# Six slots for expert tiles and three for second-layer weights, with the tile loop unrolled by six

## What is computed

```
h = tok(x)                            # 16-step patches, stride 8: 92 tokens a sample, width 128
h = h + attn(layernorm(h))            # 8 heads, keys and queries 64 wide, values 128 wide
t = layernorm(h)                      # over the 128 values of a token
gates = softmax(t @ Wr + br)          # 8 experts, the best 2 kept, scaled to a sum of 1
for e in range(8):
    out += combine[:, e] * (relu(t @ W1[e] + b1[e]) @ W2[e] + b2[e])    # hidden width 512
h = h + out
```

## Time and profile before

| | us |
|---|---|
| median of three runs | 1813.76 |
| the three runs | 1808.7 to 1816.97 |
| the profiled execution | 1818.27 |
| its span, first to last instruction | 1816.4 |

### The profile page before, as it was taken

How to read it: one execution, slowest core, us unless ns; L and a number is a source line. 1 busy time by engine, 2 the same in 40 slices (tenths; PEclk the granted TensorE clock), 3 DMA queues, 4 the chain that set the end, 5 groups by cost and what they waited for, 6 DMA issues and landing times.

```text
span 1816.4 us, 33518 instructions
## 1 busy us (share of the span) xinstructions
PE 1560.2 (86%) x8364; PEld 1258.9 (69%) x8364; DVE 1166.5 (64%) x2839; ACT 1050.4 (58%) x2345; POOL 767.5 (42%) x884
## 2 busy tenths in 40 slices
PE   6689999999999999999878889889668888888840
PEld 4568887888788878887667677767546667666630
DVE  3557888788888888888756665655535555455532
ACT  2457777777777777777645555454334444444410
POOL 1453333333333332333266555555625455455444
PEclk9889999999999999999987887887779999999975
DMA  3312222222222222222375445445246556566558
GB/s 75 105 63 76 79 75 91 75 79 75 91 75 79 75 91 75 79 75 83 134 260 185 157 166 187 168 155 185 69 166 206 199 199 209 194 209 207 189 185 299
DMA packets 144102, 247.31 MB, mean 136 GB/s; under 512 B 23856, under 2 KB 86976, under 8 KB 144064
## 3 DMA queue, kind: packets, MB, share of 16 engines
q1 hardware_dynamic: 112784, 204.37, 32.1%
q0 software_dynamic: 15008, 34.34, 5.6%
q10 hardware_dynamic: 16272, 8.15, 1.6%
HBM read 100.78 MB, written 90.43 MB: 105 GB/s over the span
## 4 chain that ended last, share of the span: by engine, by line
PE 54%; issue 15%; DVE 10%; POOL 9%; DMA 7%; ACT 3%; SPq 2%; another core or an unknown queue 0%; POOLq 0%; DVEq 0%; ACTq 0%
PE bank L308 11%; PE bank L310 9%; PE bank L309 9%; PE bank L1338 6%; PE bank L1400 4%; PE bank L1268 4%; PE bank L1366 3%; DMA w2t<-w2s 2%; POOL y_scratch L691 2%; DMA y_scratch<-ytok,tin 2%; POOL rstdA L565 2%; POOL sorted_scratch L663 1%; DVE aT_l L1060 1%; PE bank L1259 1%; DVE total L1007 1%
## 5 line engine op out<-in xcount | busy, mean ns | idle before, releaser
L558 POOL TENSOR_TENSOR prob<-expo,inv 92x368 f32<-92x368 f32 x256 | 205.0, 801 | 520.7 <-DVE inv L1017 520.7
L691 POOL DMA_INDIRECT y_scratch<-ytok,tin x212 | 202.9, 957 | 231.8 <-DVE ytok L1222 154.8
L1213 DVE SCALAR_TENSOR_TENSOR hid_l<-bank,hid_h 128x512 fp32r<-128x512 f32 x212 | 146.2, 691 | 190.0 <-ACT hid_h L902 119.7
L902 ACT ACTIVATE hid_h<-bank 128x512 fp32r<-128x512 f32 x212 | 126.2, 598 | 205.9 <-PE bank L310 156.9
L663 POOL DMA_INDIRECT sorted_scratch<-trow,posi x184 | 180.7, 982 | 145.2 <-DVE posi L1139 87.4
L1338 PE MATMUL bank<-z,xnT 128*92 128x368 f32 x512 | 203.2, 479 | 0.0
L1060 DVE TENSOR_TENSOR aT_l<-bank,aT_h 128x512 fp32r<-128x512 f32 x184 | 125.8, 691 | 113.0 <-ACT aT_h L839 84.4
L1041 DVE TENSOR_TENSOR w2s<-bank,w2s 128x368 fp32r<-128x368 f32 x256 | 136.8, 534 | 69.6 <-ACT w2s L794 69.6
L1012 DVE TENSOR_REDUCE peak<-bank 92x4 f32<-92x368 f32 x256 | 136.1, 532 | 69.6 <-PE bank L1338 69.4
L839 ACT ACTIVATE aT_h<-bank 128x512 fp32r<-128x512 f32 x184 | 109.0, 598 | 120.7 <-PE bank L1400 118.4
L785 ACT ACTIVATE expo<-cent 92x368 f32<-92x368 f32 x256 | 129.9, 507 | 74.9 <-DVE cent L1022 66.0
(11 more groups left out here) (187 smaller groups left out, 4031.4 us busy)
## 6 DMA issues: line engine op xcount, KB each, us to landing
ax_scratch<-val SPq DMA_DIRECT2D x64, 736.0 KB, 3.7
arow<-ax_scratch SPq DMA_DIRECT2D x23, 2048.0 KB
w2t<-w2s SPq DMA_DIRECT2D x53, 512.0 KB
tin<-sorted_scratch SPq DMA_DIRECT2D x53, 260.0 KB
w1t<-w_h SPq DMA_DIRECT2D x53, 256.0 KB
w1t<-w_l SPq DMA_DIRECT2D x53, 256.0 KB
xin<-in_x_dram SPq DMA_DIRECT2D x32, 372.0 KB
yin<-y_scratch SPq DMA_DIRECT2D x46, 256.0 KB, 4.4
```

Of the source, the lines that this page charges most:

```text
L558: nc.gpsimd.tensor_tensor(prob[:, k % 2], expo[:, k % 2], inv[:, k % 2].unsqueeze(2).to_broadcast([S, HH, S]), ALU.mult).then_inc(prob_kep ...
L691: pool.indirect_dma_start(out=y_dram, out_offset=bass.IndirectOffsetOnAxis(ap=tin[:, b, r, D:D + 1].bitcast(I32), axis=0), in_=ytok[:, b % ...
L1213: V.scalar_tensor_tensor(hid_l[:, f], hid_ps[f][:], 0.0, hid_h[:, f].bitcast(F32), ALU.max, ALU.subtract).then_inc(hidl_kept, 1)
```

## The change

tin gets six slots (XRING = 6) and w2t three (WRING = 3). The constants in the waits follow. SP's order in a step n becomes w2t of n+2, tin of n+3, w1t of n+2, and one more w2t and one more tin are loaded ahead of the loop. tin's load waits for the scatter of the tile six before, w2t's for the second layer three before. With XRING the unrolling changes too: 6 steps, 7 turns of 6, and 5 + 1 steps after. w1t keeps two slots, the column ring b2t has six.

```diff
-XRING = 4
+XRING = 6
+WRING = 3
...
-        w2t = sb("w2t", [P, 2, WB], F32R, stack=third)
+        w2t = sb("w2t", [P, WRING, WB], F32R, stack=third)
...
-                at_least(sp, part_done, FC * (n - 1))
-                sp.dma_start(w2t[:, q % 2].bitcast(F32), w2s[:].rearrange("p e n -> p (e n)")[:, bass.ds(e * WB, WB)].bitcast(F32)
-                             ).then_inc(w2_in[q % 2], 16)
+                at_least(sp, part_done, FC * (n - WRING + 1))
+                sp.dma_start(w2t[:, q % WRING].bitcast(F32), w2s[:].rearrange("p e n -> p (e n)")[:, bass.ds(e * WB, WB)].bitcast(F32)
+                             ).then_inc(w2_in[q % WRING], 16)
...
-                at_least(sp, y_out[q % 2], 16 * TR * (2 * i + q // 2 - 1))
+                at_least(sp, y_out[q % 2], 16 * TR * (XRING // 2 * (i - 1) + q // 2 + 1))
...
             for n in (0, 1):
                 load_w1(n, n)
                 load_w2(n, n)
+            load_w2(2, 2)
...
             load_tile(0, 0, 0)
             load_tile(1, 0, 1)
+            load_tile(2, 0, 2)
 
             def tile(n, i, q):
-                if not isinstance(n, int) or n + 2 < TILES:
-                    load_tile(n + 2, i + (q + 2) // XRING, (q + 2) % XRING)
-                if not isinstance(n, int) or 2 <= n + 1 < TILES:
-                    load_w2(n + 1, q + 1)
+                if not isinstance(n, int) or 3 <= n + 2 < TILES:
+                    load_w2(n + 2, q + 2)
+                if not isinstance(n, int) or n + 3 < TILES:
+                    load_tile(n + 3, i + (q + 3) // XRING, (q + 3) % XRING)
                 if not isinstance(n, int) or n + 2 < TILES:
                     load_w1(n + 2, q + 2)
```

More of the change, by code:

```diff
@@ L286, in build @@
         tile_in = [sem(f"tile_in{i}") for i in range(XRING)]
-        w1_in, w2_in = ([sem(f"{n}{i}") for i in (0, 1)] for n in ("w1_in", "w2_in"))
+        w1_in = [sem("w1_in0"), sem("w1_in1")]
+        w2_in = [sem(f"w2_in{i}") for i in range(WRING)]
         xt_done, xh_kept, xl_kept = (sem(n) for n in ("xt_done", "xh_kept", "xl_kept"))
@@ L1491, in first_layer @@
                     at_least(pe, xl_kept, n + 1)
-                    at_least(pe, w1_in[b], 48 * (2 * i + q // 2 + 1))
+                    at_least(pe, w1_in[b], 48 * (XRING // 2 * i + q // 2 + 1))
                 at_least(pe, hidl_kept, FC * (n - 1) + f + 1)
@@ L1500, in second_layer @@
                     at_least(pe, yT_kept, n - 1)
-                    at_least(pe, w2_in[b], 16 * (2 * i + q // 2 + 1))
+                    at_least(pe, w2_in[q % WRING], 16 * (XRING // WRING * i + q // WRING + 1))
                 at_least(pe, hidl_kept, FC * n + f + 1)
-                high, low = (w2t[:, b, (2 * f + half) * D:(2 * f + half + 1) * D] for half in (0, 1))
+                high, low = (w2t[:, q % WRING, (2 * f + half) * D:(2 * f + half + 1) * D] for half in (0, 1))
                 three(y_ps[b][:], high, low, hid_h[:, f], hid_l[:, f], f == 0, f == FC - 1).then_inc(part_done, 1)
```

## The result

| | before | after |
|---|---|---|
| median, us | 1811.23 | 1747.04 |
| runs | 1806.35 to 1816.97 (4) | 1746.68 to 1753.9 (4) |
| the profiled execution | 1818.27 | 1746.68 |
| its span | 1816.4 | 1744.9 |

The ratio is 0.9653, 95% interval 0.9614 to 0.9693: faster by 64 us, where 60 were forecast. The forecast of 1754 and its range hold for this comparison. The record doesn't name the chip of the first result.

A forecast was written before the change was run, and what follows sets the result against it. A latency ring through GpSimd's scatters and the tin and w2t loads was taken to bound the tile loop. Extra load 1.5 less 61.5 gained gave -60 us: 1758 on the profiled scale, 1754 on the runs', range 1743 to 1773.

The forecast's parts named there:

- The ring through the scatter: Tile loop before: last scatter, tin issue, w2t, second layer, next scatters form a ring of 14.85 us over two tiles.
- The next bound: Tile loop after: TensorE binds at 6.60 us a tile, 343.2 against 404.7 us, a gain of 61.5.
- the 6.46 end of the sum: Tile loop at the best tile's 6.46 us throughout: a gain of 68.8 us, used for the range's fast end.
- One more load ahead of the loop: Start of the tile stage: w2t for tile 2, issued ahead of the first tin, costs 1.5 us, up to 3.2.
- The clock, inside the gain: Tile stage: second-layer matmuls at half clock, up to 628 ns, go with the waits; counted inside the 61.5 us.
- Unrolling by six costs nothing: Tile loop: engines' loops turn 7 times instead of 11 with the same work, at no cost.
- rival B: Tile loop: an instruction fetch at each of seven turns, 6.2 us each, gives back 43 us: 1797; chance 0.04.
- Rival A: Tile loop: small waits on tin and hid_l remain, 13.1 us, so 6.85 a tile: 1767 us; chance 0.20.
- C: Second layer: hid_l is the true cause of the stalls, only 1.5 us of extra issue remains: 1815; chance 0.03.
- D: SP's queue: w1t, last, is held behind tin waiting for a scatter; slower by 18 us, 1832; chance 0.03.
- its chance of slower, 0.03: Whole kernel: 0.03 that the change makes it slower, through w1t held behind tin on SP's queue.

The follow-up runs named there:

- e1: Kernel before with w2t issued ahead of tin on SP's queue, no slots added; 1785.77 us, ratio 0.9859 to the kernel before.
- e2: Changed kernel with w2t back at two slots and behind tin, six tin slots kept; 1745.23 us, ratio 0.9633 to the kernel before.
- e6: Kernel before with a 900-column GpSimd fill ahead of each tile's four scatters; 1846.02 us, ratio 1.0154 to the kernel before.
- e4: Kernel before with every tile step written out, no loop; 1812.15 us, ratio 0.9993 to the kernel before.
- e9: The changed kernel itself, nothing edited, run again in a later batch; 1828.96 us, ratio 1.0058 to the kernel before.
- e3: Kernel before with three w2t slots, four tin slots, w2t behind tin, tile steps written out; 1799.07 us, ratio 0.9925 to the kernel before.
- e5: Changed kernel with every tile step written out, no loop; 1806.07 us, ratio 0.9932 to the kernel before.
- e7: Changed kernel with a 900-column GpSimd fill ahead of each tile's four scatters; 1772.53 us, ratio 0.9753 to the kernel before.
- e8: Changed kernel with tile 1's w1t and w2t issued behind the first two tins, tile 2's w2t behind the third; 1823.45 us, ratio 1.0036.
- e12: Changed kernel with a 450-column GpSimd fill ahead of each tile's scatters; 1795.97 us, ratio 0.9906 to the kernel before.

## Why the prediction was right, and where it was not

**The ring through the scatter: right.** e1 removes the wait on w2t without any slot; e2 removes both waits with tin's slots alone; e6 makes the scatter later and the kernel before pays 29 us. What failed is the share: I gave w2t's slot and order a part of the gain, and it has none once tin has six.

**The next bound, "for an undisturbed tile I take not the best, 6.46, but 6.60": too high.** The mean of a clean tile and one of 6.72 took in a start-up effect. Fifty intervals of 52 took 6.44 to 6.48. 52 x 6.47 is 336.4 where I had 343, so the tile stretch gave 68.3 and not 61.5. That is the 6.46 end of the sum (68.8).

**Part of the 68.3 belongs to the trace of before, and the near hit is partly luck.** In that trace TensorE's signals come late too: eight hidden blocks start over 0.5 us after all that they wait for has ended, 10.4 us in all. e4, a kernel of the same time, has no such block and took 398.55 from first to last turn, 6.2 less than the earlier trace rows. Between these two traces without late blocks, the change is worth 398.55 - 336.37 = 62.2 in that stretch. That compares single executions, and e4 spends 86.0 us behind its last turn where the kernel before spends 81.3, for no known reason. On the scale of the profiled execution the sum said 1758 and the kernel took 1746.68, 11.6 less: 6.8 for the length of a tile, 4.2 for the start, 0.5 behind the last turn. The forecast of 1754 missed by 7 only because 4.5 were taken off for the profiled execution of before, which lay that far above its median; the one of after lies 0.4 below its own.

**One more load ahead of the loop, 1.5 us: right.** From SP's first issue for the tiles to the first turn it is 12.81 us (1314.88 to 1327.69) where the trace of before has 12.00 (1318.41 to 1330.41), and that would make it 0.8. But SP's issues in that trace are odd there, as in the pauses of e9. In traces without this, the code of before takes 10.96 (e1) and 10.93 (e4). With the third w2t alone, e3 takes 12.43, 1.5 more than e4; the changed kernel takes 1.8 more than e2 (10.99), which lacks only that load. What the sum had wrong is the sign at the first turn: it came 2.7 earlier and not 1.5 later, since SP reached that point 3.5 earlier.

**The clock, inside the gain: right.** The longest of the matmuls shown took 398 ns, 628 before. The prediction read only the last of a group's three matmuls. The first of a second-layer group (L308, L310 after), right behind the wait, took 473 ns in the median and 787 at most before; from 1338 us on it takes 397 and 484 in the kernel after.

**Unrolling by six costs nothing: right.** No interval at a turn of the loop stands out, and e4 shows 0.9993 without any loop. This speaks against rival B here. The Trainium skill ("Runtime: NRT & Kernel Launch", Instruction fetch mechanics) expects a stall at a taken branch out of the fetched pages; the trace after shows none in seven turns. Nor do fetches make the pauses of e9: both pages list the same packets.

```profile
q8 instruction: 17, 0.28, 0.1%
q14 instruction: 25, 0.20, 0.0%
```

**Rival A, a remainder of waits:** not there in the result, 1.4 us in all. **C** fell with e1. **D**, w1t held behind tin: not there in the changed kernel, whose tin issues have no wait to pass on, but e3 shows the mechanism 28 times. It is what a third slot for w2t alone runs into.

**What the prediction missed altogether.** It had no case in which the same program is fast in one batch and not in another, and its chance of slower, 0.03, was for another mechanism. It took the time of a tile as a thing that the kernel alone sets, and had no term for a signal from TensorE that comes late. The kernel before took 1813 to 1820 in all four batches, the changed one 1747 or 1829. One could think that the late signals are the same for both and that the 1.3 us of idle time a tile in the kernel before swallow part of them. The traces say more: the delays themselves grow. In e6 (the kernel before with its fill) 71 of 408 recorded increments of TensorE are over 0.3 us late, up to 2.1; on the same chip e5, e7 and e8 have 144 of 402, 133 of 396 and 181 of 429, up to 4.9, 3.4 and 5.9. Why is not shown.

**What stays open.** What makes TensorE's signals and SP late is not shown. One thing narrows it: in e9 no increment of TensorE is over 0.01 us late in the first 862 us, where TensorE is nearly as dense (814 of 862 us in the earlier trace rows; all 1443 are recorded); in 862 to 1327, where GpSimd's row scatters begin, 23 of 437 are over 0.3 us late, up to 0.9, and in the tiles 172 of 426. Two accounts are left, and both fit this.

- *Scatters in a row.* In e9, with 1.26 us counted for each, GpSimd's scatters fill 0.83 of ScalarE's 24 idle stretches of 2.9 us and more ahead of hidden blocks, against 0.63 of the loop as a whole, and over half of the 24 end in or right behind a row of seven or eight scatters. No such row stands in e7 or e12. Against it: e12 has nine tiles over 9 us all the same, and in the trace of the result the scatters fill 0.78 of the loop (5.04 of 6.47 us) and nothing is late. The rows of eight can also be what a pause leaves behind, two tiles' scatters at once.
- *The recording.* The trace of the kernel after holds 14526 records of DMA landings, that of e9, the same program, 7788. e1 to e4 are full too; e5 to e12 and the trace of the kernel before have lost about half. So lost records and late signals come in the same traces, without an exception in fourteen, and in the same stages: up to 862 us e9 has 1760 landings where the trace of the result has 1776, and from 862 to 1327 2072 where that one has 4287. The Trainium skill ("NOTIFIC — the notification-queue block", section 7.1) says that a record can be dropped when software doesn't drain its queue, but that the block's internal pipeline holds the producer back rather than lose one, and so could throttle an engine. No run here shows that it did, and whether the pauses would be there without a profile is not known.

A second run of e2 and of the changed kernel together on each of the four chips would be the next step; it wasn't tried.

## What to carry to other kernels

A load that waits for a slot holds up everything behind it on its queue: give slots to the tile whose release is latest (here the one that a scatter still reads), and look only then at the one whose wait the profile names. A ring over two tiles passes on about half of what is added to it (29 of 45 us in e6), and that makes a cheap test of whether something lies in it. A wait put down to "issue" may be a load whose landing the profile didn't match: look at the last load of the tile that the instruction reads first. And run the changed kernel itself in every batch: ratios to the kernel before looked comparable across batches, and three experiments were read wrongly until the control was there.

## What the hardware showed that was not expected

- One program, two times: 1747.04 and 1828.96, each steady over its executions (1746.68 to 1753.9 and 1822.3 to 1842.85), while the kernel before moved from 1811 to 1820.
- TensorE's increment of a semaphore can stand 5.6 us behind the end of its matmul, and an idle ScalarE starts 0.03 us after the increment. The profile calls the releaser "remote" in a program on one core. That name is worth a look in any trace: 62.8 us of it stood in e9, none in the trace of the result.
- More work went with less time: e7, with 45 us of fills on GpSimd, had no tile over 8.0 us on a chip where e5 and e8, variants without the fill, had ten and twelve over 9. The changed kernel alone was not run there.
